# Batch 2's shared expert moved behind the routed tiles; low parts first and one subtraction on another engine at the start of the second attention

## The reference

```
# attention: 16 heads of 128, decaying linear attention, gate, RMS norm, projection
# FFN, for each of the 2048 tokens h (256 wide):
logits = h @ gate_w.T                              # 8 experts
two best experts, weights by softmax over their logits
routed = sum over the two: weight * (silu(h @ w1[e, :, :176]) * (h @ w1[e, :, 176:])) @ w2[e]
shared = (silu(h @ sw1.T) * (h @ sw2.T)) @ sw3.T    # 176 wide, all tokens
x = x + gate * (routed + shared)
```

## Time and profile before

| | us |
|---|---|
| runs | 1178.83 median of 3 (1176.25 to 1179.16) |
| the profiled execution | 1185.24 |
| its span, first to last instruction | 1183.4 |
| PE busy | 1069.6 (90%) |
| DVE busy | 918.9 (78%) |
| ACT busy | 734.4 (62%) |
| POOL busy | 337.7 (29%) |
| second attention stage | about 262 to 991 |
| experts ahead of the tiles | about 991 to 1065 |
| tiles | about 1065 to 1153 |
| behind the tiles | about 1153 to 1183 |

### The profile page before, as it was taken

How to read it: one execution, slowest core, us unless ns; L and a number is a source line. 1 busy time by engine, 2 the same in 40 slices (tenths; PEclk the granted TensorE clock), 3 DMA queues, 4 the chain that set the end, 5 groups by cost and what they waited for, 6 DMA issues and landing times. The chain is left out here.

```text
span 1183.4 us, 21636 instructions
## 1 busy us (share of the span) xinstructions
PE 1069.6 (90%) x7268; PEld 917.4 (78%) x7268; DVE 918.9 (78%) x1859; ACT 734.4 (62%) x1390; POOL 337.7 (29%) x347
## 2 busy tenths in 40 slices
PE   6879787777999999999999999999999997769994
PEld 5645555556888998899889988998999886659992
DVE  6688888846778878788778778788788788777775
ACT  5668686766567566666666666666666654625650
POOL 3375454443311111101111111111111244743440
PEclk9989898978999999999999999999999998879997
DMA  7210000109504004004004003004001000453436
GB/s 276 71 45 10 15 6 15 41 22 81 118 1 126 10 2 125 9 9 116 9 9 116 9 9 116 9 9 116 9 13 33 1 1 27 141 175 100 127 91 222
DMA packets 62326, 72.16 MB, mean 61 GB/s; under 512 B 21842, under 2 KB 49618, under 8 KB 61235
## 3 DMA queue, kind: packets, MB, share of 16 engines
q1 hardware_dynamic: 58850, 61.90, 19.9%
q0 software_dynamic: 3408, 9.39, 2.1%
HBM read 36.39 MB, written 32.78 MB: 58 GB/s over the span
## 5 line engine op out<-in xcount | busy, mean ns | idle before, releaser
L1475 PE MATMUL all_psum<-all_h_parts,attn_wp 128*128 128x512 f32 x1140 | 296.7, 396 | 0.0
L1647 ACT CAST attn_pp<-attn_p 128x512 fp32r<-128x512 f32 (+3 forms) x256 | 117.4, 458 | 200.8 <-DVE attn_p L1746 198.7
L1475 PEld LDWEIGHTS all_psum<-all_h_parts,attn_wp 128*128 128x128 f32 x1140 | 209.4, 189 | 39.6
L1883 POOL TENSOR_TENSOR all_gate<-all_gate,attn_sq 128x512 f32<-128x512 f32 x64 | 84.8, 1325 | 496.3 <-ACT attn_sq L1658 496.2
L1727 DVE TENSOR_TENSOR attn_pp<-attn_p,attn_pp 128x512 fp32r<-128x512 f32 (+3 forms) x256 | 200.1, 782 | 8.6 <-ACT attn_pp L1647 8.6
L1554 PE MATMUL all_psum<-attn_qkp 128*128 128x512 f32 (+3 forms) x768 | 164.6, 323 | 7.7 <-DVE attn_qkp L1727 7.7
L1501 PE MATMUL all_psum<-attn_pp,attn_vp 128*128 128x512 f32 (+3 forms) x768 | 163.2, 321 | 1.1 <-DVE attn_pp L1727 0.6
L1501 PEld LDWEIGHTS all_psum<-attn_pp,attn_vp 128*128 128x128 f32 x768 | 128.9, 189 | 21.6 <-issue 1.4
L1554 PEld LDWEIGHTS all_psum<-attn_qkp 128*128 128x128 f32 x768 | 124.4, 190 | 16.4 <-DVE attn_qkp L1727 6.2
L1746 DVE TENSOR_TENSOR attn_p<-all_psum,attn_mask 128x512 f32<-128x512 f32 (+3 forms) x256 | 123.7, 483 | 6.6 <-PE all_psum L1554 5.4
L1003 DVE TENSOR_REDUCE front_top<-all_psum 128x2 f32<-128x256 f32 (+3 forms) x128 | 100.8, 816 | 26.5 <-PE all_psum L650 26.2
(11 more groups left out here) (375 smaller groups left out, 1844.6 us busy)
## 6 DMA issues: line engine op xcount, KB each, us to landing
expert_rows<-attn_empty SPq DMA_DIRECT2D x8, 2080.0 KB, 11.3
all_wraw<-in_w1p SPq DMA_DIRECT2D x8, 1024.0 KB, 5.9
all_yacc<-expert_rows SPq DMA_DIRECT2D x39, 130.5 KB
attn_mask<-decay_masks SPq DMA_DIRECT2D x16, 256.0 KB, 2.7
experts_wx<-expert_results SPq DMA_DIRECT2D x6, 512.0 KB, 8.3
experts_xraw<-in_wx SPq DMA_DIRECT2D x4, 608.0 KB
all_wraw<-in_wx SPq DMA_DIRECT2D x4, 608.0 KB
all_x<-in_x SPq DMA_DIRECT2D x4, 512.0 KB, 7.3
```

The costliest lines, as they stand in the source:

```text
L1475: last = nc.tensor.matmul(out, wp[:, a, k, col:col + P], hh[:, c, k, b * S:(b + 1) * S], start=(m == 0), stop=(m == 5))
L1647: nc.scalar.copy(pp[:, u % 2, 0, cols], p[:, cols]).then_inc(p_hi, 1)
L1883: nc.gpsimd.tensor_tensor(cols, cols, sq[:, h, :], ALU.add).then_inc(summed, 1)
```

## The change

Three places.

1. In the attention's first lines on DVE, the low halves of the first k and q come before the last batch's attention output and statistics.
2. `post.lower(..., 0)` goes from POOL (unit 1, after `pool_biased`) to DVE (unit 1, after `qk_low(0, ...)`).
3. In the experts stage, `LATE` is 4: both quarters of batch 2 go behind the tiles as well. They accumulate in `T_BANK` (free by then), batch 3's in `Y_BANK`; gates and ups of a quarter alternate with the down of the one before. Batch 2's routed results are now added by PE against the identity too, as batch 3's. The lists of calls ahead of the tiles are written anew: the steps of the routing come earlier, the shared expert's later. The last output ahead of the tiles is batch 1's.

```diff
@@ attention, DVE
+                qk_low(1, -1, 0)
+                qk_low(0, -1, 0)
                 post.vector_attended(nc, dve)
                 post.vector_stats(nc, dve, 0)
-                qk_low(1, -1, 0)
-                qk_low(0, -1, 0)
...
                         if more:
                             qk_low(0, u, it)
+                        if first and u == 1:
+                            post.lower(dve, nc.vector, 0)
                         scores_low(u, 2, it)
@@ attention, POOL
                             post.pool_biased(nc, pool)
-                            post.lower(pool, nc.gpsimd, 0)
@@ experts
-        LATE = FS * (B - 1)
+        LATE = FS * (B - 2)
@@ SP
-                done = PARTS[:-1] + [slice(NT - TB, NT - 2), slice(NT - 2, NT)]
+                done = PARTS[:3] + [slice(tt, tt + 2) for tt in range(2 * TB, NT, 2)]
@@ down(c)
-                    if b and f == 0:
+                    if b == 1 and f == 0:
                         pe.wait_ge(upd_done, b)
-                            last = nc.tensor.matmul(ps[:, Y_BANK + tt // 2, tt % 2 * D:(tt % 2 + 1) * D],
+                            last = nc.tensor.matmul(ps[:, (T_BANK if b == 2 else Y_BANK) + tt // 2, tt % 2 * D:(tt % 2 + 1) * D],
@@ PE behind the tiles
-                pe.wait_ge(upd_done, B - 1)
+                pe.wait_ge(upd_done, B - 2)
...
                 ups(LATE)
-                gates(LATE + 1)
-                ups(LATE + 1)
-                down(LATE)
-                down(LATE + 1)
-                pe.wait_ge(results_in[B], 32)
-                for half in range(2):
...
+                for c in range(LATE + 1, FS * B):
+                    gates(c)
+                    ups(c)
+                    down(c - 1)
+                down(FS * B - 1)
+                for b, at_bank in ((2, T_BANK), (B - 1, Y_BANK)):
+                    pe.wait_ge(results_in[b + 1], 32)
+                    for half in range(2):
+                        for c in range(2):
+                            tt = b * TB + 2 * half
+                            last = nc.tensor.matmul(bank(at_bank + half), t["ident"][:, :],
+                                                    results[:, c, tt:tt + 2, :].rearrange("p t n -> p (t n)"),
+                                                    start=False, stop=(c == 1))
+                        last.then_inc(pair_made, 1)
@@ ACT behind the tiles
                 silu(LATE)
-                silu(LATE + 1)
-                high(LATE)
-                high(LATE + 1)
+                for c in range(LATE + 1, FS * B):
+                    silu(c)
+                    high(c - 1)
+                high(FS * B - 1)
@@ DVE behind the tiles
+                hide(LATE)
+                lower(LATE)
+                hide(LATE + 1)
+                add_results(0)
+                lower(LATE + 1)
+                hide(LATE + 2)
+                add_results(1)
+                lower(LATE + 2)
+                hide(LATE + 3)
+                lower(LATE + 3)
+                add_results(2)
+                for i, (b, half) in enumerate([(b, half) for b in (2, 3) for half in range(2)]):
...
```

More of the change, by code:

```diff
@@ L2446, in _ @@
                 token_rows(2, 0)
-                down(0)
+                gates(2)
+                rank(2)
                 token_rows(2, 1)
-                rank(2)
-                down(1)
+                ups(1)
                 logits(3)
@@ L2453, in _ @@
                 turn_logits(3)
+                ups(2)
+                token_rows(3, 1)
+                rank(3)
+                down(0)
+                route.tensor_count(nc, pe, bank(ROUTE_BANK))
+                down(1)
                 gates(3)
                 ups(3)
-                token_rows(3, 1)
-                rank(3)
-                gates(4)
-                route.tensor_count(nc, pe, bank(ROUTE_BANK))
-                ups(4)
                 down(2)
-                gates(5)
                 down(3)
-                ups(5)
-                down(4)
-                down(5)
                 for e in range(E):
@@ L2533, in _ @@
                 ups(LATE)
-                gates(LATE + 1)
-                ups(LATE + 1)
-                down(LATE)
-                down(LATE + 1)
-                pe.wait_ge(results_in[B], 32)
-                for half in range(2):
-                    for c in range(2):
-                        tt = (B - 1) * TB + 2 * half
-                        last = nc.tensor.matmul(bank(Y_BANK + half), t["ident"][:, :],
-                                                results[:, c, tt:tt + 2, :].rearrange("p t n -> p (t n)"),
-                                                start=False, stop=(c == 1))
-                    last.then_inc(pair_made, 1)
+                for c in range(LATE + 1, FS * B):
[12 more added lines that the diff above has]
+                        last.then_inc(pair_made, 1)
             @block.scalar
@@ L2822, in _, with add_results @@
                 dve.wait_ge(hid_turned, TILES)
-                hide(LATE)
-                hide(LATE + 1)
-                lower(LATE)
-                lower(LATE + 1)
-                for i, part in enumerate(PARTS[:4]):
+                def add_results(i):
+                    part = PARTS[i]
                     dve.wait_ge(results_in[i], 32)
```

131 lines of the change are left out of this document (60 added, 71 removed).

## The result

Twenty runs of the changed kernel have their median at 1174.66 us (1171.33 to 1175.98), twenty of the kernel before at 1178.52. The ratio is 0.9964, 95% interval 0.995 to 0.9978: some 4.2 us faster, beyond the 0.3% that the prediction took as the least change to be told. One slow execution of the kernel before, at 1236.8 us, is not in this ratio. I had forecast 10.8 us less than the median shown, at 1168.

A forecast was written before the change was run, and what follows sets the result against it. TensorE was taken as the limit in both steady loops, so only three stretches around them could move. Terms 5.0 (attention), 5.0 (ahead of tiles) and 0.7 (tail) took 10.7 off 1185.24: 1174.5, less 6.4 for plain runs: 1168, range 1162 to 1176.

The forecast's parts named there:

- Edit 3: Ahead of the tiles: batch 2's shared expert moved behind them and a new order start tile 0 5.0 us earlier (1.2 to 6.5).
- the scatter chain: Ahead of the tiles: routing slots, metadata, GpSimd's scatters, then row loads; scatters and row loads were to come 1.2 us earlier.
- The other chain: Ahead of the tiles: VectorE's work from batch 3's slots to the last gating out of PSUM, ending at 1059.4, 5.0 us earlier.
- Edit 1: Start of the second attention: low halves of k and q ahead of the post work, 3.0 us gained (2.3 to 3.7).
- the "2.9": Ahead of the tiles: of 3.7 us less VectorE work before batch 3's slots, 2.9 kept as the slots' gain.
- The collision: Start of the attention: VectorE's sum into x slides into GpSimd's weight subtractions and may lose about 1.4 us.
- Edit 2: Attention: post batch's low half on VectorE instead of GpSimd; PE starts 1.2 us earlier, plus 0.8 (0 to 1.7) for its clock.
- Edit 4: Tail: batch 2's shared expert fits PE's wait for results, 16 identity matmuls replace 8; 0.7 us gained (-5 to +1.5).
- (b): Ahead of the tiles: only the scatters' 1.2 us is gained because VectorE is stopped again; 6.9 in all, 1172 us; chance 0.2.
- (c): Tail grows: late quarters and results don't interleave, down(7) 2 us late, 16 matmuls cold, +5 instead of -0.7; 1174 us; chance 0.12.
- (d): Tail: PE falls to 1.2 GHz and stays there, tail ends 17.5 us later, net 7 slower, 1186 us; chance 0.05.
- (e): Whole change does next to nothing: attention gains given back, early tile start eaten by the tail; 1177 us; chance 0.08.

The follow-up runs named there:

- e14: Changed kernel with batch 3's metadata directly behind its slots, and last lower and output ahead of later weight subtractions: ratio 0.9951 to the kernel before.
- e16: Changed kernel with batch 3's metadata directly behind its slots and its tanh early: 1171.71 us, ratio 0.9949 to the kernel before.
- e1: The kernel before, unchanged, profiled a second time: 1179.18 us.
- e3: The kernel before with the attention edits alone (low halves first, post batch's low half on VectorE): ratio 0.9938 to the kernel before.
- e17: The kernel before with the attention edits alone, on another chip: 1170.64 us, ratio 0.9946 to the kernel before.
- e4: The kernel before with the experts' edits alone (batch 2's shared expert behind the tiles, new order), attention as before: ratio 1.0007 to the kernel before.
- e2: The changed kernel, unchanged, profiled a second time: 1170.68 us.
- e12: The changed kernel, unchanged, on a third chip: median 1175.79 us, ratio 0.9934 to the kernel before.
- e11: The kernel before with the attention edits alone, on the third chip: median 1177.77 us, ratio 0.9942 to the kernel before.
- e9: The kernel before, unchanged, a third profiled execution, on the third chip: 1185.43 us.
- e7: Changed kernel with batch 3's metadata directly behind its slots on VectorE and its tanh ahead of weight copies on ScalarE: ratio 0.9926 to the kernel before.
- e5: The kernel before with only the two low halves of k and q moved ahead of the post work: ratio 0.9956 to the kernel before.
- e15: The changed kernel, unchanged, on a fourth chip: ratio 0.9949 to the kernel before.
- e10: The kernel before with GpSimd's scatters of batch 2 held until batch 3's slots are made: 1185.02 us.
- e6: The kernel before with only the post batch's low half moved to VectorE: ratio 0.999 to the kernel before.

## Why the prediction was wrong

**The step that failed** is Edit 3, in "the scatter chain": "1042.9, scatters from 1043.1, 1.2 earlier. Row loads: 1056.5", and behind it "The row loads' 1.2 allow it: their first row had time to spare". The last scatter came later in the new order, not earlier: at 59.3 to 61.7 where nothing was held (old order 57.8 to 59.6), at 63.9 where it was (61.3 to 61.7), so by some 2 us. And the row loads' spare time was that execution's own. In every profile of the new order but e14 and e16 tile 0 starts 4.8 to 5.2 us behind the last scatter: that is the row loads' pace. In the profile that I read it was 10.4 behind, so 5.4 us of room; in e1 and e3 there were 2.0 and 1.7, in e17 0.2. Removing the third output could give what was left of this room, and the later scatters took that away. The other chain was too large in the sum as well: the last gating ahead of the tiles, forecast 5.0 us earlier, came 2.3 to 3.2 earlier beside runs of the same chip (e4 63.77 against e1 66.10, e2 61.41 against e3 63.99, e12 66.03 against e11 69.00 and e9 69.18), and not at all in e16 against e17.

The changed kernel shows it. SP's timeline, the first row load, and PE's, the first tile:

```profile
1051.74 3.64 SPq L2342 DMA_DIRECT2D all_yacc<-expert_rows  x4
```

```profile
1053.98 0.66 PE L2473 MATMUL all_psum<-all_ident,all_yacc 128*128 128x128 f32 x2 [4.29 <-DMA all_yacc<-expert_rows]
1054.95 0.69 PE L2473 MATMUL all_psum<-all_ident,all_yacc 128*128 128x128 f32 x2 [0.31 <-DMA all_yacc<-expert_rows]
```

PE waits for rows here, where before it waited for the output of the earlier trace rows. VectorE's last gating out of PSUM had ended at 1050.95, 3 us earlier. PE transposes tile 1, too, before the first hidden product, and waits for its rows as well (the second bracket). So from the first transposes to that product it takes 2.0 to 2.3 us in the changed kernel, and 1.5 (in e17 1.7) in the old order where an output was waited for. And PE is cold: its granted clock was 0.50 through the wait and at the first hidden products, as this window shows.

```profile
1050.00:1058.00 8.00, 3.36 (x11) 2.54 (x12) 3.02 (x4) 0.75 (x2) 0.00 (x0) 0.50 0.33 86
```

From the first hidden product to the last tile's down product the two profiles at 1.00 there (e3, e17) took 86.6 to 86.7 us, nine with the clock low for a part of the first 4 us 87.8 to 88.0, and the eight at 0.50 for all of them 88.5 to 88.9. So the clock at the start of the tiles is worth another 2.3 us, which no term of my sum has.

**Two things made the scatters late**, and I could have counted both. First, the metadata. I let the last group of scatters follow slots(3) by 2.0 us (1041.1 to 1043.1); it took 5.0. Not all of that is lost, since GpSimd was busy with the group before for 3.4 of it: where the old order ran without held waits (e1, e3, e17) the last group followed that one after 0.30 us, a scatter's usual step, so there the slots did not set its start at all, and the 2.82 us of waiting that I read belonged to the held execution. In the changed kernel this gap is 1.60 us (e2 1.31, e4 3.13). The group then began 1.4 us earlier (e2 against e3) to 0.2 us later (e4 against e1), for slots 4.7 and 4.4 us earlier. VectorE's timeline of the changed kernel:

```profile
1030.79 0.17 DVE L2093 CAST experts_slot<-experts_slotf 128x8 int32<-128x8 f32 x1
1032.07 1.43 DVE L2684 TENSOR_TENSOR experts_wx<-experts_xraw,experts_wx 128x1216 fp32r<-128x1216 f32 x1 [1.11 <-ACT experts_wx L2551]
1034.78 0.17 DVE L2053 COPY experts_rows_out<-experts_best_idf 128x8 f32<-128x8 f32 x1 [1.28 <-ACT experts_lead L2045]
```

The subtraction waits for the high part of a weight that lands late, and the metadata for a tanh that stands on ScalarE behind the next such copy. Moving a step behind another makes it inherit what that one waits for. Second, weight subtractions now run under the scatters. GpSimd's timeline, the first and the last two of batch 3, and VectorE's beside those two:

```profile
1035.94 2.15 POOL L2855 DMA_INDIRECT expert_rows<-experts_rows_out,experts_slot  x1 [1.60 <-issue]
...
1044.93 2.01 POOL L2855 DMA_INDIRECT expert_rows<-experts_rows_out,experts_slot  x1 [0.30 <-issue]
1047.25 1.63 POOL L2855 DMA_INDIRECT expert_rows<-experts_rows_out,experts_slot  x1 [0.30 <-issue]
```

```profile
1044.69 1.42 DVE L2684 TENSOR_TENSOR experts_wx<-experts_xraw,experts_wx 128x1216 fp32r<-128x1216 f32 x1
...
1046.62 1.42 DVE L2684 TENSOR_TENSOR experts_wx<-all_wraw,experts_wx 128x1216 fp32r<-128x1216 f32 x1
```

A scatter that begins behind such a subtraction ends 0.83 to 0.84 us behind it (1046.11 to 1046.94, 1048.04 to 1048.88), instead of lasting 0.96. The first of the group meets one as well (1035.83 to 1037.25) and lasts 2.15. The eight take 12.9 us in all (60.81 less a start at 47.87), against 9.9 to 11.0 in the old order; this, more than the start, is the step that failed. I had weighed just this collision for Edit 1 and not for the scatters. The Trainium skill, "SBUF — State Buffer", section "Who interferes with whom", says that a software DMA stalled by a VectorE operation is GpSimd starved of port time for its descriptors; the rows agree that the scatter waits for VectorE's operation. The same section infers that a `tensor_tensor` does not stall such transfers, and these subtractions are of that kind (TENSOR_TENSOR in the rows), so on this point the measurement decides. The order of e7, e14 and e16 takes the first cause away, e14's part of the second, too (its eight take 11.1 us), and the last scatter comes 2 us or more earlier (held: 61.72 and 61.18 against 63.85 and 63.95; not held: 56.78 against 59.34 to 61.69).

**How it passed unnoticed.** I wrote of a wait of over 3 us at the ranks "I cannot explain that wait", and carried it over. I read one execution, 6.4 us above the median, and took that off at the end as a constant. It was no constant: the earlier trace rows holds part of it, in the stretch that I predicted, and of the 5.4 us of room that the term of 5.0 needed, 3.4 or more were made by those waits (e1 had 2.0). Two smaller slips stand beside it. The lower bounds of edits 1 and 2 add up to 3.5 us, not to 3.0. And the "2.9" that I kept of 3.7 has no working in the text; beside runs of the same chip the slots did come 2.1 to 4.7 us earlier.

**Edit 1**, forecast 3.0 (2.3 to 3.7): 3.5 us (e5). First scores 4.0 earlier (forecast 4.1), transposes 3.55 (3.7). The collision cost less than the 1.4 that I had feared. In the changed kernel's timelines, GpSimd's weight subtractions and VectorE's sum into x, the sum takes half a microsecond more than its 1.23 alone. It began 0.68 us before GpSimd's second subtraction ended (273.88), and lost no more than this rest; that the loss had to be all of 1.4 or nothing was my mistake.

```profile
271.90 1.98 POOL L1875 TENSOR_TENSOR attn_wp<-all_wraw,attn_wp 128x512 fp32r<-128x512 f32 x2 [2.09 <-ACT attn_wp L1611]
```

```profile
273.20 1.76 DVE L295 TENSOR_TENSOR all_x<-all_x,all_yacc 128x1024 f32<-128x1024 f32 x1
```

**Edit 2**, forecast 1.2 and 0.8 for the clock (0 to 1.7): 1.2 and 0.3 or 1.5. The gap was 1.96 us (forecast 1.9). Half of 1.7 as the mean of two cases was not far from what thirteen profiles give (1.5 in nine of them, about 0.3 in four). Both edits together: 5.0 forecast, 5.0 to 6.5 found in the stage (e2, with the slower last pair, 5.2), 6.4 to 7.3 in the three timed comparisons (e3, e11, e17).

**Edit 4**, forecast 0.7 gained (−5 to +1.5): nothing. The tail lasts 29.1 to 29.2 us in every profile of the new one, and 27.6 to 29.8 in nine with the old, their middle at 29.03. The steps on PE were right. PE's timeline: down(7) ends as the identity matmuls begin, 18.2 us behind the last tile's product (1143.80; forecast 17.5), and 16 of them take 7.03 us, 0.44 each (forecast 7.1), at the full clock:

```profile
1162.03 7.03 PE L2539 MATMUL all_psum<-experts_wx,all_ident 128*128 128x512 f32 x16
```

PE has no wait for the results left, where it waited 9.3 to 10.5 us before. In the old tail the eight identity matmuls began 18.0 to 19.2 us behind the last tile's product and took 5.2 to 6.7 us; now the sixteen begin at 18.2 and take 7.03 in every profile, so the new tail is bound by PE and no longer varies.

**The rivals.** (b), that the stretch gains only what the scatters gain, was the right kind, and even its 1.2 us was too much. (c) did not occur, as down(7) was 0.7 us late and not 2, and the matmuls ran at the full clock. (d) did not either; the gaps of 0.5 us before the downs left the clock at 1.00 (1144 to 1162). (e) named the tail as what eats the early start; what ate it lay ahead of tile 0. Together: attention 5.0 to 6.5 gained; up to tile 0's hidden product 0.6 to 0.7 lost where nothing is held (e2 against e3, e4 against e1) and 0 to 0.2 gained where it is (e12 against e11 and e9); tail 0. That makes 4.3 to 6.7 us, against 4.2 in the first comparison and 7.8 and 6.0 in e12 and e15. These are parts of single executions, and what the clock does in the tile loop (up to 2.3 us) and in the old tail (2.2 us) is not in them.

## What to carry to other kernels

Before a stall without a releaser goes into a sum, take a second execution: what differs between two of the same kernel is no room that an edit can claim. When the last item of a stretch is removed, list every chain that ends there with the distance of each to the end (in e3 output, row loads and weights would have let tile 0 start within 2 us of each other), because the gain is the distance to the next one. Where GpSimd issues a group of indirect transfers, VectorE operations with two SBUF inputs belong in front of or behind the group, not beside it. And a reordering that frees one chain can lengthen another, as e14's did.

## What the runs showed of the hardware

VectorE went on up to 5.8 us behind the end of PE's rows (1039.56 to 1045.33 in e9) while a group of scatters ran, and only in some executions: it waited 0.8 to 4.55 us at rank reads in twelve profiles, not at all in the seven others. Holding the scatters back moved the wait with them (e10). Its mechanism is open.

A scatter that begins while a 128x1216 subtraction with two SBUF inputs runs on VectorE ends 0.83 to 0.84 us behind it (1046.11 to 1046.94 in the changed kernel) instead of lasting 0.96 us.

The product behind an idle gap of 1.96 us took 3.1 us, as at the full clock, in nine profiles of thirteen, and 4.2 to 4.3 in four; behind 3.1 us it took 4.6 in all six. Behind another idle gap, of 1.95 us, the granted clock of the next 5 us was 0.66 in e2 and e6 and 1.00 in the seventeen others.
